# Attention scores as 64-row matmuls of two heads in turn, with units of half a batch's queries

## The reference

```python
q_hk = (hidden_q @ Wq.T).reshape(b, s, H, K)              # hidden_q = layernorm(x)
q_big = einsum('bshk,hkq->bshq', q_hk, w_kc_q)
kv_rope = kv_c * cos + rotate_half(kv_c) * sin
q_r = einsum('bshq,hqr->bhsr', q_big, W_qr)
k_r = einsum('bld,hdr->bhlr', kv_rope, W_kr)
scores = einsum('bhsr,bhlr->bhsl', q_r, k_r)               # contraction over R = 64
ctx_c = einsum('bhsl,bld->bhsd', softmax(scores), kv_rope)
ctx_lat = einsum('bhsd,hkd->bshk', ctx_c, w_kc_kv)
x = x + tanh(g_xattn) * (ctx_lat.reshape(b, s, H * K) @ Wo.T)
x = x + tanh(g_ffn) * ffn(layernorm(x))                   # three quantized products, silu gate
```

## Time and profile before

| | us |
|---|---|
| runs: median (lowest to highest of 3) | 853.43 (852.34 to 854.44) |
| profiled execution, its span | 853.0 |
| TensorE busy | 756.1 (89%) |
| weight loads busy | 550.0 (64%) |
| VectorE busy | 667.7 (78%) |
| ScalarE busy | 538.0 (63%) |
| GpSimd busy | 242.7 (28%) |
| share of the chain that ended last: PE, DVE, issue, ACT | 53%, 21%, 12%, 9% |

### The profile page before, as it was taken

The page is one execution under the profiler, slowest core; times in us unless marked ns, Lnnn a source line. Parts: engine busy times, 40 slices in busy tenths (PEclk is TensorE's granted clock), DMA queues, the critical chain, the costliest instruction groups (busy, mean ns, idle before and its releaser), DMA issues.

```text
span 853.0 us, 12547 instructions
## 1 busy us (share of the span) xinstructions
PE 756.1 (89%) x3792; PEld 550.0 (64%) x3792; DVE 667.7 (78%) x1083; ACT 538.0 (63%) x873; POOL 242.7 (28%) x224
## 2 busy tenths in 40 slices
PE   2768998999999999998999999999989987868896
PEld 2555776777687778776867686767766765424443
DVE  4865867686677767776898889888989896879984
ACT  1576767677676867674657566656565655458775
POOL 1421213121312222222222222222222224377751
PEclk9879999999999999998999999999999998899999
DMA  7301040104010401040104110310122110000001
GB/s 231 136 1 50 25 135 26 51 25 136 25 49 25 135 28 60 19 139 14 50 26 136 36 38 25 135 49 25 35 70 75 54 70 2 1 1 13 25 25 38
DMA packets 24976, 47.66 MB, mean 56 GB/s; under 512 B 6000, under 2 KB 11248, under 8 KB 24816
## 3 DMA queue, kind: packets, MB, share of 16 engines
q1 hardware_dynamic: 23904, 46.01, 16.1%
q10 hardware_dynamic: 976, 1.25, 0.4%
q0 software_dynamic: 64, 0.00, 0.0%
HBM read 45.16 MB, written 2.10 MB: 55 GB/s over the span
## 4 chain that ended last, share of the span: by engine, by line
PE 53%; DVE 21%; issue 12%; ACT 9%; POOL 2%; DMA 1%; DVEq 0%; ACTq 0%; POOLq 0%; SPq 0%
PE ps_s L925 8%; PE ps_b L957 7%; PE ps_b L900 7%; DVE et_lo L1195 4%; DVE small L1231 4%; PE ps_ctx L935 4%; PE ps_ctx L937 4%; PE ps_ctx L936 4%; DVE k_st L1195 3%; PE ps_s L453 3%; PE ps_b L912 3%; PE ps_b L914 2%; PE ps_b L913 2%; ACT k_st L1053 2%; PE ps_b L483 2%
## 5 line engine op out<-in xcount | busy, mean ns | idle before, releaser
L825 POOL TENSOR_SCALAR E<-E,small 128x1024 f32<-128x1024 f32 x128 | 151.0, 1180 | 503.9 <-DVE small L1236 490.1
L1053 ACT ACTIVATE et_hi<-ps_b 128x512 fp32r<-128x512 f32 x256 | 152.7, 597 | 156.9 <-PE ps_b L957 156.3
L1195 DVE TENSOR_TENSOR et_lo<-ps_b,et_hi 128x512 fp32r<-128x512 f32 x256 | 175.7, 688 | 74.9 <-ACT et_hi L1053 70.7
L925 PE MATMUL ps_s<-k_st,q_st 128*128 128x512 f32 x512 | 152.6, 422 | 19.2 <-ACT E L1086 11.9
L957 PE MATMUL ps_b<-ident,E 128*128 128x128 f32 x1024 | 156.1, 275 | 14.6 <-DVE k_st L1195 9.2
L1086 ACT ACTIVATE E<-ps_s,small 128x1024 f32<-128x1024 f32 x128 | 142.9, 1117 | 33.8 <-DVE small L1231 32.8
L957 PEld LDWEIGHTS ps_b<-ident,E 128*128 128x128 f32 x1024 | 127.1, 141 | 55.7 <-DVE k_st L1195 9.2
L1231 DVE TENSOR_REDUCE small<-ps_s 128x1 f32<-128x1024 f32 x128 | 155.4, 1215 | 5.7 <-PE ps_s L925 5.1
L935 PE MATMUL ps_ctx<-et_hi,kv_hi 128*128 128x512 f32 x256 | 118.2, 462 | 4.2 <-DVE et_lo L1195 2.2
L925 PEld LDWEIGHTS ps_s<-k_st,q_st 128*128 128x128 f32 x512 | 91.8, 195 | 41.7 <-ACT E L1086 18.9
L937 PE MATMUL ps_ctx<-et_lo,kv_hi 128*128 128x512 f32 x256 | 102.1, 399 | 0.0
(11 more groups left out here) (145 smaller groups left out, 1052.7 us busy)
## 6 DMA issues: line engine op xcount, KB each, us to landing
w_stage<-in_wffn SPq DMA_DIRECT2D x48, 512.0 KB, 3.5
wo_s<-in_woT SPq DMA_DIRECT2D x8, 512.0 KB, 5.6
wq_s<-in_wq SPq DMA_DIRECT2D x7, 512.0 KB, 5.6
wkcq_s<-in_wkcqT SPq DMA_DIRECT2D x7, 384.0 KB, 4.0
x_sb<-in_x SPq DMA_DIRECT2D x4, 512.0 KB, 7.0
out<-x_sb SPq DMA_DIRECT2D x8, 256.0 KB, 2.0
wqr_s<-in_wqr SPq DMA_DIRECT2D x7, 192.0 KB, 4.3
E<-in_ctx SPq DMA_DIRECT2D x2, 512.0 KB, 9.0
```

Of the source, the lines that this page charges most:

```text
L825: nc.gpsimd.tensor_scalar(e, e, rowinv[:, k:k + 1], 1.0, ALU.mult, ALU.mult).then_inc(scaled, 1)
L925: last = nc.tensor.matmul(ps_s[:, t % 2, cols], q_st[:, h, part, t * P:(t + 1) * P], k_st[:, b, h, cols], start=(part == 0), stop=(part == 1))
L1053: return nc.scalar.activation(out, in_, ACT.Copy)
L1195: return nc.vector.tensor_tensor(out, full, hi.bitcast(F32), ALU.subtract)
```

## The change

The unit becomes half of a batch's queries for both heads: its four tiles are two query tiles s x two heads h. Scores are computed for both heads at once, in steps 0 and 3: with three products (hi x hi, hi x lo, lo x hi), each a matmul of 64 rows, that alternate between head 0 (rows 0 to 63, first half of `ps_s`) and head 1 (rows 64 to 127, second half). `k_st` and `q_st` give way to `k_hi`, `k_lo`, `q_hi`, `q_lo`, whose rows are both heads' 64; k and q tasks copy and subtract all 128 rows at once, and `double_queries` goes. Maxima come in steps 0, 1, 3 and 4, exponentials in 1, 2, 4 and 5, inverses in 2, 3, 5 and 6. "out" (u, s) needs only unit u and can run one unit later; two instead of four are left for the feed-forward's first step. The side tasks get new steps.

```diff
-SCORE_STEP = {0: 0, 1: 1, 2: 2, 3: 3}
-EXP_STEP = {s + 1: t for s, t in SCORE_STEP.items()}
-INV_STEP = {s + 2: t for s, t in SCORE_STEP.items()}
+HEADS_AT_ONCE = 2
+SCORE_STEP = {0: 0, 3: 1}
+MAX_STEP = {0: 0, 1: 1, 3: 2, 4: 3}
+EXP_STEP = {s + 1: t for s, t in MAX_STEP.items()}
+INV_STEP = {s + 2: t for s, t in MAX_STEP.items()}
-DOUBLE_STEP = 7
 SIDE = [
-    {4: ("out", 1, 0), 5: ("q", 1), 6: ("out", 1, 1), 7: ("out", 1, 2)},
-    {0: ("out", 1, 3), 2: ("m",), 4: ("a",), 5: ("b", 0), 6: ("b", 1)},
-    {2: ("k", 0, 0), 3: ("k", 0, 1), 4: ("out", 0, 0), 5: ("q", 0), 6: ("out", 0, 1), 7: ("out", 0, 2)},
-    {0: ("out", 0, 3), 3: ("k", 1, 0), 5: ("k", 1, 1)},
+    {2: ("q", 1), 4: ("out", 3, 0), 5: ("out", 3, 1), 7: ("b", 0)},
+    {0: ("b", 1), 1: ("m",), 4: ("out", 0, 0), 5: ("out", 0, 1), 6: ("k", 0, 0), 7: ("a",)},
+    {1: ("k", 0, 1), 2: ("q", 0), 5: ("out", 1, 0), 6: ("out", 1, 1)},
+    {2: ("k", 1, 0), 4: ("out", 2, 0), 5: ("out", 2, 1), 7: ("k", 1, 1)},
 ]
-SIDE_LAST = {2: {4: ("out", 0, 0), 5: ("out", 0, 1), 6: ("out", 0, 2), 7: ("out", 0, 3)}, 3: {}}
+WK_AT = (1, 1)
...
-        k_st = sa("k_st", [P, BATCH, 2, LCTX], F32R)
-        q_st = sa("q_st", [P, 2, 2, SEQ], F32R)
+        k_hi = sa("k_hi", [P, BATCH, LCTX], F32R)
+        k_lo = sa("k_lo", [P, BATCH, LCTX], F32R)
+        q_hi = sa("q_hi", [P, BATCH, SEQ], F32R)
+        q_lo = sa("q_lo", [P, BATCH, SEQ], F32R)
...
-        def score_matmuls(pe, p, w, t):
-            if not (is0(p) and w == 0 and t < 2):
-                pe.wait_ge(exp_done, 16 * p + (4 * w + t - 1))
-            b, h = divmod(w, 2)
+        def score_matmuls(pe, p, w, s):
+            if not (is0(p) and w == 0 and s == 0):
+                pe.wait_ge(exp_done, 16 * p + (4 * w + 2 * s))
+            b, half = divmod(w, 2)
+            rows = slice((2 * half + s) * P, (2 * half + s + 1) * P)
             for j in range(2):
                 cols = slice(j * NF, (j + 1) * NF)
-                for part in range(2):
-                    last = nc.tensor.matmul(ps_s[:, t % 2, cols], q_st[:, h, part, t * P:(t + 1) * P],
-                                            k_st[:, b, h, cols], start=(part == 0), stop=(part == 1))
-            last.then_inc(scores_done, 1)
+                for i, (q, k) in enumerate(((q_hi, k_hi), (q_hi, k_lo), (q_lo, k_hi))):
+                    for h in range(HEADS_AT_ONCE):
+                        head = slice(h * R, (h + 1) * R)
+                        last = nc.tensor.matmul(ps_s[:, h, cols], q[head, b, rows], k[head, b, cols],
+                                                start=(i == 0), stop=(i == 2))
+                        if j == 1 and i == 2:
+                            last.then_inc(scores_done, 1)
...
             if kind == "k":
                 _, b, j = task
                 cols = slice(j * NF, (j + 1) * NF)
-                copy_act(k_st[0:R, b, 0, cols], bank_in[0:R, :])
-                last = copy_act(k_st[R:P, b, 1, cols], bank_in[R:P, :])
+                last = copy_act(k_hi[:, b, cols], bank_in)
             elif kind == "q":
-                copy_act(q_st[0:R, 0, 0, :], bank_in[0:R, :])
-                last = copy_act(q_st[R:P, 1, 0, :], bank_in[R:P, :])
+                last = copy_act(q_hi[:, task[1], :], bank_in)
...
-        def double_queries(act, n):
-            act.wait_ge(side_freed, n)
-            copy_act(q_st[R:P, 0, :, :], q_st[0:R, 0, :, :])
-            copy_act(q_st[0:R, 1, :, :], q_st[R:P, 1, :, :]).then_inc(q_doubled, 1)
...
-                lo_part(k_st[R:P, b, 0, cols], bank_in[0:R, :], k_st[0:R, b, 0, cols])
-                last = lo_part(k_st[0:R, b, 1, cols], bank_in[R:P, :], k_st[R:P, b, 1, cols])
+                last = lo_part(k_lo[:, b, cols], bank_in, k_hi[:, b, cols])
             elif kind == "q":
-                lo_part(q_st[0:R, 0, 1, :], bank_in[0:R, :], q_st[0:R, 0, 0, :])
-                last = lo_part(q_st[R:P, 1, 1, :], bank_in[R:P, :], q_st[R:P, 1, 0, :])
+                last = lo_part(q_lo[:, task[1], :], bank_in, q_hi[:, task[1], :])
```

More of the change, by code:

```diff
@@ L74 @@
 SIDE = [
-    {4: ("out", 1, 0), 5: ("q", 1), 6: ("out", 1, 1), 7: ("out", 1, 2)},
[3 rows of a table removed]
[4 rows of a table added]
 ]
-SIDE_LAST = {2: {4: ("out", 0, 0), 5: ("out", 0, 1), 6: ("out", 0, 2), 7: ("out", 0, 3)}, 3: {}}
+WK_AT = (1, 1)
 def side_tasks(w, first, last):
     def wanted(task):
-        before = task[:2] == ("out", 1)
+        before = task[:2] == ("out", 3)
         behind = task[0] in ("m", "a", "k") or task == ("q", 0)
         return not (first and before or last and behind)
-    side = SIDE_LAST.get(w, SIDE[w]) if last else SIDE[w]
-    return {c: task for c, task in side.items() if wanted(task)}
+    return {c: task for c, task in SIDE[w].items() if wanted(task)}
 PROLOGUE_TASKS = [("m",), ("a",), ("q", 0), ("k", 0, 0), ("k", 0, 1), ("k", 1, 0), ("k", 1, 1)]
@@ L456, in step @@
                     if isinstance(t, int) and t == 0 and c == 0:
-                        for s in range(ST):
+                        for s in range(2):
                             pe_last_out(pe, s)
@@ L576, in ln2_stats @@
             if i < 2:
-                dve.wait_ge(side_freed, side_index(7, "last", ("out", 0, tiles[-1])) + 1)
+                dve.wait_ge(side_freed, side_index(7, "last", ("out", i, 1)) + 1)
             else:
@@ L860, in _, with out_matmuls @@
             ffn_pool(pool)
+        def out_matmuls(into, u, s):
+            for h in range(2):
+                cols = slice((2 * s + h) * P, (2 * s + h + 1) * P)
+                nc.tensor.matmul(into, ctx_hi[:, u % 2, cols], b_hi[:, h, :], start=(h == 0), stop=False)
+                nc.tensor.matmul(into, ctx_lo[:, u % 2, cols], b_hi[:, h, :], start=False, stop=False)
+                last = nc.tensor.matmul(into, ctx_hi[:, u % 2, cols], b_lo[:, h, :], start=False, stop=(h == 1))
+            return last
         def side_matmuls(pe, p, variant, task, into, at=None):
@@ L906, in side_matmuls @@
             else:
[L907 to L914, removed]
[L915 to L921 removed]
+                _, u, s = task
+                pe.wait_ge(ctx_done, 4 * p if u == 3 else 4 * p + u + 1)
+                last = out_matmuls(into, u, s)
+            last.then_inc(side_done, 1)
+        def score_matmuls(pe, p, w, s):
[3 more added lines that the diff above has]
+            rows = slice((2 * half + s) * P, (2 * half + s + 1) * P)
             for j in range(2):
                 cols = slice(j * NF, (j + 1) * NF)
[L924 to L927 removed]
+                for i, (q, k) in enumerate(((q_hi, k_hi), (q_hi, k_lo), (q_lo, k_hi))):
[5 more added lines that the diff above has]
+                            last.then_inc(scores_done, 1)
         def pv_matmuls(pe, p, w, c):
@@ L982, in pe_last_out @@
                 pe.wait_ge(ctx_done, UNITS)
[L983 to L991, removed]
+                pe.wait_ge(side_freed, LAST_SIDE)
+            out_matmuls(ps_b[:, s % 3, :], 3, s).then_inc(side_done, 1)
         @block.tensor
@@ L1025, in _ @@
             pe.wait_ge(side_freed, 5)
[L1026 to L1031, removed]
+            score_matmuls(pe, 0, 0, 0)
+            turn_kv(2)
+            turn_kv(3)
+            score_matmuls(pe, 0, 0, 1)
             turn_x(ST, ps_ctx)
@@ L1121, in act_pair @@
                         side_high(act, p, variant, tasks[c], ps_b[:, bank(w, c, 1), :])
-                    if c == 5 and w == 1 and variant != "last":
+                    if (w, c) == WK_AT and variant != "last":
                         wk_high(act, 16 * p + 32)
@@ L1126, in act_pair @@
                         g += 1
-                    if c == DOUBLE_STEP and (w == 0 or w == 2 and variant != "last"):
-                        double_queries(act, side_index(p, variant, ("q", 1 - w // 2)) + 1)
                     if variant == "last":
@@ L1282, in dve_pair @@
                         side_low(dve, p, variant, tasks[c], ps_b[:, bank(w, c, 1), :])
-                    if c in SCORE_STEP and scores:
-                        max_tile(dve, *next_unit(p, w), SCORE_STEP[c])
-                    if c == 5 and w == 1 and variant != "last":
+                    if c in MAX_STEP and scores:
+                        max_tile(dve, *next_unit(p, w), MAX_STEP[c])
+                    if (w, c) == WK_AT and variant != "last":
                         wk_low(dve, p + 2)
```

21 lines of the change are left out of this document (10 added, 11 removed).

## The result

| | before | after |
|---|---|---|
| runs, median (lowest to highest), us | 853.75 (852.34 to 854.44, 4) | 888.56 (886.87 to 889.40, 4) |
| profiled span, us | 853.0 | 887.6 |
| until the first pair's transposes | 53.1 | 52.4 |
| pairs 0 to 3 (sums) | 329.5 | 336.0 |
| pairs 4 to 6 (quantization) | 256.7 | 283.0 |

The ratio is 1.0415 (1.0397 to 1.0433); 821.5 had been forecast, in 803 to 868. The stages run from a pair's first transposes to the next one's, the rest from the last transposes on. They say where it went: +26.3 us in the three quantizing pairs, +8.7 in the last, +6.5 in four summing ones, -0.7 before and -6.2 behind.

What follows compares the result with a forecast made beforehand. TensorE's stream was taken to set each pair, VectorE close behind where it quantizes. Start -5.5, pairs 0 to 3 -15.2, pairs 4 to 6 -7.5, last pair -1.5 and end -2.0 took 853.0 to 821.3, forecast 821.5, range 803 to 868.

Steps and rivals of the forecast that it cites:

- Side by side: Score groups: neighbouring 64-row matmuls on different row halves overlap, so 12 fill six slots, 1.38 us.
- One after another: Rival on score groups: row halves don't overlap, a group costs 2.76 us, total 879 (864 to 895); chance 0.20.
- The passages: Going between 128-row and 64-row matmuls around each score group costs 0.16 us, making a group 1.54 in place of 1.84.
- Dear switch: Rival: side by side, but both passages pay drain and load, a group 2.08 us, total 852 (838 to 862); chance 0.18.
- side estimate of 1.79 us a group: Score group if two tiles reached 77% of their ideal, as four 32-row tiles do in the notes; sum near 835.
- The copies: k and q tasks: half the copies and subtractions, 4.1 us less on VectorE a pair, shorter k chains; 3.8 taken.
- The new wait at step 3: Second score group waits for both exponentials of the first: 1.0 us in unit 1, 1.4 in unit 3, 2.4 a pair.
- the sum of the standing: TensorE's idle time: 1.4 us less in a summing pair; with the cheaper scores, quantizing pairs gain only 2.5.
- The plan binds: Rival: step 3 waits in all units or VectorE's backlog after step 5 stays, 2.7 us more a pair, about 841; chance 0.05.
- The start: Before the pairs: fewer copies and subtractions -3.2 and -1.8, scores side by side -0.5, together -5.5 us.
- The end and the last pair: Output products moved out of the feed-forward's first step, -2.0 us; fewer score tiles in the last pair, -1.5.

Runs made afterwards that it cites:

- e12_same_rows: Changed kernel with both heads' score matmuls on rows 0 to 63, order and count kept, so none can run side by side: 1020.73 us, ratio 1.1951.
- e13_split_copies: Changed kernel with refitted order, side tasks and weight halves (836.9 us), its k and q copies and subtractions split into 64 rows each again: 865.71 us, ratio 1.0153.
- e14_inverse_only: Changed kernel with one edit, on VectorE the inverse ahead of the wait for et_hi of its step: 872.52 us, ratio 1.0232.
- e10_better: Changed kernel with VectorE's maxima and inverses earlier, side tasks and weight halves moved, k (1, 1) at step 6 of unit 3: 836.86 us, ratio 0.9806.
- e9_fit6: Changed kernel with VectorE order, side tasks and weight halves refitted (846.43 us), then 6 score matmuls of 128 rows a group for 12 of 64: 825.01 us, ratio 0.9677.
- e2_full6: Changed kernel, its plan kept, with 6 score matmuls of 128 rows a group in place of 12 of 64 rows: 877.94 us, ratio 1.0277.
- e3_one_head_first: Changed kernel with the same 12 score matmuls, the six of head 0 first and then the six of head 1: 932.87 us, ratio 1.0923.

## Why the prediction was wrong, by its steps

**Side by side: right.** The couples start 3 ns apart and six slots are filled. "One after another" gave 879, near the measured 888.6, and is nevertheless wrong in its mechanism: e12_same_rows shows what it costs, 1020.7.

**The passages: the mechanism right, the size too small.** 0.16 us a group was taken; the trace has 0.42, so a group is 1.80 and not 1.54, and the gain is 0.04 in place of 0.30, 0.3 us a pair in place of 2.4. Over 62 groups that is 16 of the 66 us between the forecast span (821.3) and the measured one (887.6). I took the value near the passage from products to transposes, which isn't a change of rows and showed nothing of one. The Trainium skill, TensorEngine Tiling (Array Packing), Key Properties, has the drain at each change of tiling, and both passages here agree with it (0.20 and 0.19 us). "Dear switch" was right in kind and priced too high (2.08). That the prediction's side estimate of 1.79 us a group meets the measured 1.80 is luck: it put the loss into the packing, where there is none (six slots in 1.41). And the loads were no bound on a group, as the prediction argued from twelve in a row, since those of a couple start together.

**The copies: right.** A copy of 128x512 takes 602 ns and a subtraction 681 in after, half as many as in the earlier trace rows:

```profile
L1184 DVE TENSOR_TENSOR k_lo<-ps_b,k_hi 128x512 fp32r<-128x512 f32 x4 | 2.7, 681 | 0.2 <-ACT k_hi L1053 0.2
...
L1053 ACT ACTIVATE k_hi<-ps_b 128x512 fp32r<-128x512 f32 x4 | 2.4, 602 | 0.4 <-PE ps_b L902 0.3
...
L1184 DVE TENSOR_TENSOR q_lo<-ps_b,q_hi 128x512 fp32r<-128x512 f32 x2 | 1.4, 691 | 3.5 <-ACT q_hi L1053 3.5
```

VectorE's busy time came out at 55.7 and 71.2, as forecast (56, 71.2), and e13_split_copies prices it at 3.8 us in a summing pair, as was taken. It was the change's real gain, though the 3.8 of e13_split_copies is measured in a plan with the k tasks at other steps.

**The new wait at step 3: nearly right.** 1.0 and 1.4 were forecast in units 1 and 3 and none in 0 and 2; steps 3 take 5.07 and 5.21 there against 3.62, so 1.5 and 1.6.

**What failed is the sum of the standing.** The prediction wrote "Net, 3.8 against 2.4: 1.4 less standing a pair" and "So I take only -2.5" for a quantizing pair. With a stream of 76.1 us (76.4 less eight times 0.04) TensorE stands for 8.0 us of the summing pair's 84.1 where it stood for 5.8, and for 14.3 of pair 6's 90.4 where it stood for 7.4. The forecast had left 4.4 and 7.3. The growth is at the steps 7. They take 3.01, 3.17, 1.51 and 3.35 us in pair 2's four units and 4.52, 4.54, 2.90 and 4.77 in pair 6's, where TensorE has 1.99, 2.92, 1.13 and 1.82 of work by the pieces of the earlier trace rows: 3.2 us of standing in pair 2 and 8.9 in pair 6, beside 3.1 and 3.3 at the steps 3. Three waits there weren't priced. (1) Side tasks at step 7 (b, a, k) wait for an et_lo behind VectorE's halves: I compared VectorE's 8 to 9 us with TensorE's 5.6 in unit 0's steps 5 to 7, and booked 1.3 us a pair for it. (2) The fourth tile's inverse, a step later, was dismissed with POOL's low busy time, while it stands in VectorE's queue behind the same half; with it moved, the steps 7 of pairs 4 to 7 lose 11 us (e14_inverse_only). (3) k (1, 1) at step 7 of unit 3 holds the bank for the next pair's first transposes; e10_better gains 1.6 us a pair by moving it. "The plan binds" was this mechanism; it had a chance of 0.05 and 2.7 us a pair, where the measured excess over the forecast was 5.7 in pair 2 and 9.1 in pair 6, 2.1 of it from the passages in each. (The forecast's last addition is 0.2 off, 821.3 + 0.4 being 821.7; it changes nothing.)

**In pair 4 the plan puts q behind the stop.** It takes 100.5 us where pair 5 takes 92.1; before, 89.1 and 83.8. So the stop costs 8.4 us in place of 5.3. All wait there for the mean of the weights. In after the next thing behind that stop is q of step 2, in the timeline of TensorE:

```profile
397.69 6.30 PE L909 MATMUL ps_b<-xnT,a_sb 128*128 128x512 f32 x8 [4.55 <-DVE et_lo L1184]
```

The clock is at its lower level of 1.2 GHz behind the idle 4.55 us, and q takes 6.30 in place of 3.45. The prediction had no term for it. (In e14_inverse_only, whose clock stays up there, q takes 3.70.)

**The start: -5.5 forecast, -0.7 measured.** The chain of after:

```profile
28.40 0.61 ACT q_hi L1053
...
31.03 2.48 DVE small L1299 x4
...
34.11 1.14 DVE small L1218
...
35.33 2.31 ACT E L1078 x4
...
37.69 2.97 PE ps_s L933 x12
```

The scores began at 31.2 and not 33.2, but VectorE's statistics of the second batch (31.03) then stand ahead of the first maximum (34.11), and the second group (37.69) waits for both exponentials (35.33). I had named no next-late step. **The end and the last pair: -3.5 forecast, +2.5 measured.** The products did move (-6.2), into a pair that grew by 8.7.

## What to carry to other kernels

Where a change re-plans the queues of several engines, book for each step what stands ahead in each engine's queue, not only the sums of busy time: here the operations got cheaper as forecast and the pair got longer. A tiny operation (an inverse of 0.15 us) behind a 2.4 us one on an in-order engine can cost 3 us in a pair of 90, and a few lines' move gives it back. Price a part (e9_fit6 against e2_full6, 21 against 11 us) in a plan with few waits, and look at the granted clock of the stretches before a saving is called covered.

## What the runs showed of the hardware that was not expected

- Two 64-row matmuls of 512 float32r columns on different row halves start 3 ns apart and fill one slot of 0.23 us, each with its own load of weights; the two loads start 4 ns apart (404.351 and 404.355 in after).
- Going from 128-row to 64-row matmuls and back takes 0.20 and 0.19 us in after, with an uncovered load each way. Six full-row matmuls in place of a group save 21 us over 62 groups in e9_fit6.
- With six matmuls of one row half queued ahead of six of the other, the other half's first starts ahead of three issued before it (e3_one_head_first, 429.639 against 429.861).
- With 64-row matmuls that don't overlap, the granted clock was 0.93 over a stretch where TensorE was busy for 94 of 100 us (e12_same_rows); after's pair 2, busy for 78 of 84, had 1.00.
